# Moving VectorE's denominators, decay factors and routing scalars into PSUM in a two-layer gated feed-forward kernel

## The reference, cut to what matters

```
tf    = sigmoid(sum(time_emb));  decay = exp(-exp(w)) * (0.5 + 0.5*tf)
ek    = exp(min(k, 30));  ekv = ek*v                  # k = v = F in both layers
nf,df = forward scan over T of (a*decay + ekv, b*decay + ek);  nb,db = the same, reversed
euk   = exp(min(u + k, 30))
num   = nf + nb - ekv + euk*v;  den = df + db - ek + euk
wkv   = sigmoid(r) * num / max(den, 1e-8) * (0.8 + 0.2*tf)
layer 0: r = x;  gate = argmax(softmax(wkv @ Wg.T)) of 8 experts
         x = x + (wkv @ A[gate].T) @ Bw[gate].T * 4 * prob
layer 1: r = x;  h = gelu(wkv @ tern(w1).T + b1);  x = x + h @ tern(w2).T + b2
```

## Time and profile before

| | us |
|---|---|
| median of 3 runs | 126.23 (126.23 to 126.68) |
| the profiled execution | 126.34 |
| its span (first to last instruction) | 124.5 |
| DVE busy | 108.2 (87%) |
| PE busy | 101.1 (81%) |
| ACT busy | 83.0 (67%) |
| POOL busy | 51.7 (42%) |

### The profile page before, as it was taken

The page is one execution under the profiler, slowest core; times in us unless marked ns, Lnnn a source line. Parts: engine busy times, 40 slices in busy tenths (PEclk is TensorE's granted clock), DMA queues, the critical chain, the costliest instruction groups (busy, mean ns, idle before and its releaser), DMA issues.

```text
span 124.5 us, 2082 instructions
## 1 busy us (share of the span) xinstructions
PE 101.1 (81%) x654; PEld 93.7 (75%) x654; DVE 108.2 (87%) x218; ACT 83.0 (67%) x148; POOL 51.7 (42%) x61
## 2 busy tenths in 40 slices
PE   5596791099987999699725999967989799989991
PEld 5485790099976889599524899956979799989990
DVE  1389999999999999999999997999999999994731
ACT  4186989940676934469248549878099996997441
...
PEclk9999689756999599999985599999999999999999
...
DMA packets 7271, 6.44 MB, mean 52 GB/s; under 512 B 2370, under 2 KB 7004, under 8 KB 7260
## 3 DMA queue, kind: packets, MB, share of 16 engines
...
...
q10 hardware_dynamic: 16, 0.00, 0.0%
...
## 4 chain that ended last, share of the span: by engine, by line
DVE 58%; PE 17%; issue 17%; DMA 2%; DVEq 1%; ACT 1%; ACTq 0%
DVE run L708 14%; DVE nd L726 11%; PE bank L1134 6%; DVE own L695 4%; PE bank L1054 4%; DVE hm L776 4%; DVE mask L768 3%; PE bank L1101 3%; DVE nd L738 3%; DVE run L716 2%; DMA vec_rows<-in_L_cond_u_dram 2%; DVE nd L250 2%; DVE h_lo L262 2%; DVE nd L236 2%; DVE nd L223 2%
## 5 line engine op out<-in xcount | busy, mean ns | idle before, releaser
L708 DVE TENSOR_TENSOR_SCAN run<-bank,kv 128x256 f32<-128x256 f32 x32 | 20.1, 669 | 0.4
L726 DVE TENSOR_TENSOR_SCAN nd<-bank,run 128x256 f32<-128x256 f32 x32 | 20.1, 673 | 0.2
L1054 PE MATMUL bank<-hm,BT 128*128 128x256 f32 x64 | 16.9, 423 | 1.5 <-DVE hm L776 1.5
L1038 PE MATMUL bank<-nd,AT 128*128 128x256 f32 x64 | 17.7, 431 | 0.0
L1101 PE MATMUL bank<-xin_hi,w1T 128*128 128x256 f32 x64 | 15.8, 287 | 1.7 <-ACT h L536 1.2
L1054 PEld LDWEIGHTS bank<-hm,BT 128*128 128x128 f32 x64 | 13.6, 217 | 4.2 <-DVE hm L776 1.9
L262 POOL TENSOR_TENSOR h_lo<-h,h_hi 128x512 fp32r<-128x512 f32 x6 | 8.1, 1348 | 20.4 <-DVE h_hi L270 14.0
L1134 PE MATMUL bank<-w2T,h_hi 128*128 128x256 f32 x64 | 15.9, 287 | 0.5 <-DVE h_lo L262 0.5
L1038 PEld LDWEIGHTS bank<-nd,AT 128*128 128x128 f32 x64 | 15.8, 330 | 0.4
L1134 PE MATMUL bank<-w2T,h_lo 128*128 128x256 f32 x64 | 15.3, 278 | 0.0
L1101 PE MATMUL bank<-xin_lo,w1T 128*128 128x256 f32 x64 | 15.2, 279 | 0.0
...
## 6 DMA issues: line engine op xcount, KB each, us to landing
...
vec_rows<-in_L_cond_w_dram ACTq DMA_DIRECT2D x2, 1.0 KB
```

Source lines behind the costliest of these rows:

```text
L708: dve.tensor_tensor_scan(run[:, r, c, q], decay_ps[:, l, c, b:b + 1].broadcast_to([P, T]), kv[:, b, c, q], 0.0, ALU.mult, ALU.add).then_in ...
L726: dve.tensor_tensor_scan(nd[:, r, c, q, ::-1], decay_ps[:, l, c, b:b + 1].broadcast_to([P, T]), run[:, r, c, q, ::-1], 0.0, ALU.mult, ALU. ...
L1038: mm = pe.matmul(bank[H_BANK + k][:, (m % 2) * T:(m % 2 + 1) * T], AT[:, c, m::NM], nd[:, r, c, NUM, :], start=(c == 0), stop=(c == NC - 1))
L1054: mm = pe.matmul(bank[y_bank[b % 2]][:, o * T:(o + 1) * T], BT[:, m, o * P:(o + 1) * P], hm[:, b % 2, m], start=False, stop=(o == NC - 1 a ...
```

## The change

The denominators move from `nd` in SBUF to whole PSUM banks, the numerators get a ring of four slots of their own, and DVE's small factors are kept in bank 5 beside the decays. The steps of the denominators that POOL had go to DVE: it does `add_den` and `den_times_rec` in all eight (l, b) and POOL takes `own_keys` and more of the numerator's steps. The sigmoid is multiplied into the numerator before the reciprocal arrives. In the last two ratios the refined reciprocal is made first (`refine_rec`) and the numerator multiplied in by `product`. `cond` is loaded from ACT's queue, ahead of w and u, which are transposed apart. `own_keys` is called by POOL alone. The orders of all four lists are new. Cut to its core:

```diff
-        nd = sb("nd", [P, RING, NC, 2, T])
+        num = sb("num", [P, NUM_RING, NC, T])
...
-        F_bank, x_bank = [0, 1, 7, 0], [2, 3, 4, 2]
-        A_bank, B_bank = [1, 7], [3, 4]
-        H_BANK, y_bank, o_bank, LAST_BANK = 0, [2, 3], [0, 1], 5
-        g_bank = [7, 4] * 4 + [2, 3, 7, 4] * 2
+        F_bank, x_bank = [0, 1, 7, 0], [2, 4, 2, 4]
+        A_bank, B_bank = [1, 2], [1, 2]
+        H_BANK, Y_BANK, o_bank, LAST_BANK = 0, 2, [0, 1], 5
+        den_bank = [3, 7, 3, 7, 3, 3, 3, 2]
+        g_bank = [7, 4] * 4 + [6, 7, 4] * 2 + [6, 7]
...
+        decay_ps, inv_gain_ps, scale_ps, cap_ps = [factor_columns(k * ND) for k in range(4)]
+        expert_ps = bank[DVE_BANK][:, EXPERT_AT:EXPERT_AT + P]
...
-                dve.tensor_tensor(last, last, inv_gain[:, l, :, b], ALU.mult).then_inc(seeded[q][r], 1)
+                dve.tensor_tensor(last, last, inv_gain_ps[:, l, :, b], ALU.mult).then_inc(fwd_steps[q][r], 1)
...
-                    dve.tensor_tensor_scan(nd[:, r, c, q, ::-1], decay_ps[:, l, c, b:b + 1].broadcast_to([P, T]),
+                    dve.tensor_tensor_scan(into[:, c, ::-1], decay_ps[:, l, c, b:b + 1].broadcast_to([P, T]),
...
+            def add_den(l, b):
+                dve.tensor_tensor(den_at(l, b), den_at(l, b), own[:, r, :, DEN, :], ALU.add).then_inc(den_ready[r], 1)
+            def den_times_rec(l, b):
+                dve.tensor_tensor(den_at(l, b), den_at(l, b), run[:, r, :, DEN, :], ALU.mult).then_inc(dr_ready[r], 1)
+            def refine_rec(l, b):
+                dve.scalar_tensor_tensor(den_at(l, b), den_at(l, b), 2.0, run[:, r, :, DEN, :], ALU.subtract, ALU.mult).then_inc(q_ready[r], 1)
+            def product(l, b):
+                dve.tensor_tensor(output_at(l, b), den_at(l, b), num_at(l, b), ALU.mult).then_inc(ratio_ready[NB * l + b], 1)
...
-                    dve.tensor_scalar(mask[:, i % (2 * NT)], expert_of[:, :], idx[:, i:i + 1], grec[:, i:i + 1], ALU.is_equal,
-                                      ALU.mult).then_inc(mask_ready, 1)
+                    dve.tensor_scalar(mask[:, i % (2 * NT)], expert_ps, bank[DVE_BANK][:, IDX_AT + i:IDX_AT + i + 1],
+                                      bank[DVE_BANK][:, GREC_AT + i:GREC_AT + i + 1], ALU.is_equal, ALU.mult).then_inc(mask_ready, 1)
...
             def expert_in(b, k):
                 if b == 0:
                     pe.wait_ge(AT_ready, NC)
                     pe.wait_ge(ek_exp, NB)
                     pe.wait_ge(vs_ready, NB)
+                    pe.wait_ge(BT_ready, 2)
...
             def weight_totals():
                 pe.wait_ge(wsum_ready, 2)
...
-            keep_warm(fwd_done[NUM][0], 2, 6)
-            keep_warm(bwd_done[NUM][0], 2, 8)
-            keep_warm(fwd_done[NUM][1], 2, 8)
-            keep_warm(bwd_done[NUM][1], 2, 8)
+            keep_warm(rec_ready[0], 1, 8)
             keep_warm(dr_ready[0], 1, 8)
```

More of the change, by code:

```diff
@@ L389, in _ @@
-            times_sigmoid(pool, 2)
+            times_sigmoid(pool, 1)
+            num_times_rec(0, 1)
+            clip_keys(pool, 3)
+            times_values(pool, 3)
+            own_keys(pool, 0, 3)
+            own_values(pool, 0, 2)
+            add_num(pool, 0, 2)
+            times_sigmoid(pool, 2)
+            own_values(pool, 0, 3)
+            own_keys(pool, 1, 1)
+            num_times_rec(0, 2)
+            add_num(pool, 0, 3)
+            own_keys(pool, 1, 0)
+            times_sigmoid(pool, 3)
@@ L401, in _ @@
-            den_times_rec(pool, 1, 1)
+            own_keys(pool, 1, 3)
+            own_values(pool, 1, 2)
+            own_values(pool, 1, 3)
             add_num(pool, 1, 1)
+            num_times_rec(1, 1)
+            h_low(pool, 0, 1)
             h_low(pool, 0, 0)
+            h_low(pool, 0, 2)
+            xin_low(pool, 1)
             h_low(pool, 0, 3)
-            xin_low(pool, 1)
+            add_num(pool, 1, 2)
+            h_low(pool, 1, 0)
+            xin_low(pool, 2)
             h_low(pool, 1, 1)
-            h_low(pool, 1, 2)
@@ new lines, in _ @@
+            add_den(0, 3)
+            gate(2)
+            backward(0, 3, NUM)
+            forward(1, 0, NUM)
+            seed(1, 0, DEN)
+            gate_index(2)
+            backward(1, 0, DEN)
+            expert_mask(2)
+            seed(1, 0, NUM)
+            add_den(1, 0)
+            den_times_rec(0, 3)
+            backward(1, 0, NUM)
+            ratio(0, 3)
+            select_expert(2, 0)
+            select_expert(2, 1)
+            gate(3)
+            den_times_rec(1, 0)
+            forward(1, 1, DEN)
@@ L839, in _ @@
+            ratio(1, 0)
+            seed(1, 1, DEN)
+            ffn_input(0)
+            backward(1, 1, DEN)
+            add_den(1, 1)
             forward(1, 1, NUM)
+            gate_index(3)
+            expert_mask(3)
+            forward(1, 2, DEN)
             seed(1, 1, NUM)
-            forward(1, 0, DEN)
-            seed(1, 0, DEN)
-            backward(1, 0, DEN)
-            clip_keys(dve, 3)
-            ratio(0, 2)
-            own_keys(1, 0)
-            select_expert(1, 0)
-            select_expert(1, 1)
@@ L849, in _ @@
-            gate(2)
-            gate_index(2)
-            backward(1, 0, NUM)
-            forward(0, 3, DEN)
-            seed(0, 3, DEN)
-            backward(0, 3, DEN)
-            expert_mask(2)
-            own_keys(1, 1)
-            add_den(dve, 0, 3)
-            forward(0, 3, NUM)
-            seed(0, 3, NUM)
-            backward(0, 3, NUM)
-            select_expert(2, 1)
-            select_expert(2, 0)
-            ratio(1, 0)
-            ffn_input(0)
-            add_num(dve, 0, 3)
@@ L895, in _ @@
-            num_times_rec(dve, 1, 2)
-            den_times_rec(dve, 1, 2)
-            ratio(1, 2)
+            forward(1, 3, NUM)
+            den_times_rec(1, 2)
+            refine_rec(1, 2)
+            product(1, 2)
+            ffn_input(2)
             h_high(dve, 1, 0)
-            ffn_input(2)
-            h_low(dve, 1, 0)
-            forward(1, 3, NUM)
+            forward(1, 3, DEN)
+            xin_high(dve, 2)
+            seed(1, 3, DEN)
+            backward(1, 3, DEN)
             seed(1, 3, NUM)
-            backward(1, 3, DEN)
@@ L904, in _ @@
-            xin_high(dve, 2)
-            xin_low(dve, 2)
-            add_den(dve, 1, 3)
+            add_den(1, 3)
+            h_high(dve, 1, 3)
+            h_high(dve, 1, 2)
             backward(1, 3, NUM)
-            add_num(dve, 1, 3)
-            h_low(dve, 1, 3)
-            den_times_rec(dve, 1, 3)
-            num_times_rec(dve, 1, 3)
-            ratio(1, 3)
+            h_low(dve, 1, 2)
+            den_times_rec(1, 3)
+            refine_rec(1, 3)
+            product(1, 3)
+            ffn_input(3)
@@ L924, in _ @@
             h_low(dve, 3, 3)
+            result(dve, 2)
             last_result(dve, 1)
```

651 lines of the change are left out of this document (334 added, 317 removed).

## The result

| | before | after |
|---|---|---|
| median, us | 126.27 (126.23 to 126.68, 4 runs) | 116.8 (116.29 to 117.3, 4 runs) |
| span of the profiled execution | 124.5 | 115.5 |
| ratio after / before | | 0.9234 (0.9201 to 0.9266) |

The change is 7.7% faster. The forecast was 112.5, in a range of 106.5 to 119.0. The profiled execution took 117.3 us, 1.8 more than its span.

A forecast was written before the change was run, and what follows sets the result against it. DVE was taken to bound the kernel, PE close behind. Start 27.8 + PE work 75.1 + half clock 1.8 + waits 3.5 = 108.2; with tail and time outside the span, 112.5 us, range 106.5 to 119.

The forecast's parts named there:

- The bound and the mechanism: DVE bounds the kernel, PE close behind; DVE's seeds and masks are stretched by standing behind POOL's running instructions.
- the first rival: DVE's stretched seeds and masks stay long, since POOL being at work causes it: 118 us, up to 120; chance 0.08.
- DVE's list: Operations leaving DVE and shorter seeds and masks bring its busy time from 108.2 to about 88 us.
- PSUM's cost: DVE's bank reads and writes taken as free; at most 0.07 us for each of some 30 wide writes, 2 us.
- POOL's own_keys: Sixteen 256-column instructions gained by POOL at 0.40 us each, upper price 0.64: +6.4 us busy.
- The walk to the first expert matmul: DVE's and ACT's work from the prologue on summed to a start at 27.8 us instead of 32.8: -5.0.
- The new wait of thresholds: DVE stands 3 to 5 us at thresholds behind PE's weight_totals; PE meets it once, some 1.6 us.
- PE's stretch: First expert matmul to PE's end: 75.1 us of work, 1.8 of half clock, 3.5 of waits.
- the range's own worst case: The forecast's slow end, 117.5 us: bank writes dear (2 us) and 3 us more of waits.
- POOL becomes late: POOL's in-order list, 13 us longer, delays the numerators of both layers: 117.6 us; chance 0.13.
- PE's clock falls: Fewer warming transposes and waits for masks put PE's eight expert groups at 1.2 GHz: 139 us; chance 0.04.
- Nothing changes: DVE's savings are all spent waiting for thresholds, ACT's late copies or the gelus: 126 us; chance 0.02.

The follow-up runs named there:

- e4: The changed kernel with seeds and masks reading their small operands from SBUF again, denominators still in banks: 116.91 us, ratio 0.926.
- e6: The changed kernel with all new operands back in SBUF, denominators included, the order of the lists and the sigmoid's place kept: 126.09 us, ratio 0.998.
- e5: The changed kernel with POOL's eight own_keys calls in different operation and operand forms, output not the reference's: one run, 113.9 us.
- e3: The changed kernel with ACT's list alone reordered, scaled_values(3), evacuate_B(1) and key_exp(3) ahead of both abs_sum and gate_exp(0): 112.06 us, ratio 0.887.
- e8: The kernel of e3 with own_keys(0,0) and own_keys(0,1) moved from POOL to DVE: 110.87 us, ratio 0.881.
- e2: The changed kernel with all eight own_keys on DVE in place of POOL: 116.76 us, ratio 0.924.
- e11: The kernel of e8 with two neighbours in POOL's list exchanged, num_times_rec(0,2) ahead of own_keys(1,1): 107.77 us, ratio 0.854.

## Why the prediction was right, and where it was wrong

**The bound and the mechanism: right.** DVE stood behind POOL, because of where a second input lay. e4 brings the long seeds back by operands alone, e6 the rest. That settles the first rival (0.08), which had the stretch stay. The rule of the Trainium skill named there, SBUF — State Buffer, section Who interferes with whom, fits the seeds and denominators, and e6 shows POOL stretched when DVE starts first. One reading was too short: PE's 10 us of idle did not all wait for DVE. By name 5.4 us did and 4.4 waited for ACT, the longest of them

```profile
66.18 0.26 PE L1078 MATMUL bank<-identb,above 128*128 128x128 bf16 x1 [2.63 <-ACT w2T L517]
```

and that copy stands in ACT's list behind a `log_den` which had waited 3.93 us for DVE's `add_den`. So this one too goes back to DVE, by way of ACT.

**DVE's list: right, a little timid.** Forecast 88 us, measured 83.4. What the forecast left as it was gave most of the difference: the casts of the expert number took 164 ns for 545 in the mean, `negmax` 156 for 446, the casts of `h_high` 423 for 633 and `h_low` 719 for 796. The seeds took 0.144 for 0.164; the masks 0.417 for 0.34. That last term was under: a mask that reads only its bank takes 418 ns at the median for 341 at best before, 0.6 us in all.

**PSUM's cost: right.** 11 ns for a scan's write (684 and 673), 19 for `add_den` against an addition in SBUF (696 for 677). The 0.07 allowed for a write was too much. The dearer access that the Trainium skill has in VectorE: DVE Perf Modes, section on the TRN2 errata, a gap of 62 cycles, an estimated 65 ns at the 0.96 GHz it gives, would fit the mask's 77 and none of the wide instructions; no run tells it from another cause.

**POOL's own_keys: the price was wrong.** "256 columns take 0.40", taken from the clip as "the same operation with constants in place of per-partition columns", was 1.22, outside the upper bound of 0.64. It was not the same operation: the clip is min with max, this is multiply with min (e5). It put 13 us onto POOL. The Trainium skill, GPSIMD Engine Reference, section on elementwise work, gives a body with "k ≤ 2" 1.03 cycles per element (read here as at most two operations on one input); an estimate from that and its 1.2 GHz, with the 0.20 us of a 16-column instruction, is 0.42. The pairs min-max and multiply-add of e5 agree, the mixed pair does not.

**The walk to the first expert matmul: wrong, the step that cost the 4 us.** It had ACT's work, 10.6 us, in one run from 17.1 with "0.6 of `gate_exp`" and no wait: 27.8. ACT began at 16.75 and worked 9.9, but waited 3.04 for the denominator that `own_keys` delayed and 4.00 in `gate_exp(0)`: 33.7, and PE at 33.86. The forecast placed `keep_warm` "until about 22"; it ran to 29.3, since it waits for a copy of B behind `abs_sum(0)`. e3 takes the order alone away and gets back 4.7 us; e8 adds the two `own_keys` for 1.2 more, and reaches 26.9. The text did say that a first expert matmul after 30 would put this walk wrong.

**The new wait of thresholds: right in size.** Forecast 3 to 5 us, measured 4.72. It was to cost PE 1.6 us until `expert_out(0)`; PE was idle for 0.1 there (41.96 to 42.10). That it costs nothing at the end is not shown: the last chain runs through `thresholds`, and no run takes this wait away.

**PE's stretch: right.** Forecast 75.1 of work, 1.8 of half clock and 3.5 of waits: 80.4. Measured 78.64: 1.4 of idle, and at a mean clock of 0.97 some 6% of it at half speed, 2.4 us lost; leaves 74.9 of work. So +6.1 at the start and -1.8 here put PE's end 4.3 us behind the forecast's 108.2. The tail was 3.0 us for 2.6, and the profiled execution lay 0.5 above the median for 0.1, so 4.3 us is also what the medians show (116.8 for 112.5). That the time stayed in the range is in part luck: the range's own worst case, 117.5, had no late start in it, and waits smaller than allowed made good a third of it.

**The other rivals.** *POOL becomes late* (0.13, 117.6) is near the measured time by its number, and its sign, DVE idle behind POOL, is there (3.43 at 20.14). But its mechanism, numerators late all along, was not what cost: without any `own_keys` on POOL the time was the same (e2), and with ACT's list mended POOL's late pieces cost 1.2 us (e8) and some 2.2 (e11). *PE's clock falls* did not come: the strip's last five ends at 37.5 us, inside `expert_in(0)`, and no group behind it ran at half clock. *Nothing changes* was 9 us off.
